# A mixture-of-experts layer: the rows of the expert slots turned by transposing DMAs instead of TensorE

## The chip, the cores and the metric

The kernel runs on one core of one Trainium2 chip. The metric is the device time of one execution in microseconds (us). The times are medians of several runs.

## The reference, cut to what matters

4096 tokens of 128 channels go through an attention-like block and a mixture of experts, each followed by a layer norm. What the change touches is the second half:

```python
x = _layernorm(x + attention(x))                      # called x1 below, [4096, 128]
logits = x @ gate_w                                   # 8 experts, 2 chosen for each token
top_v, top_i = top_k(logits, 2); top_p = softmax(top_v)
g = einsum('th,ehi->tei', x, Wg); u = einsum('th,ehi->tei', x, Wu)      # 352 inner columns
d = einsum('tei,eih->teh', silu(g) * u, Wd)
expert_out = einsum('te,teh->th', combine, d)         # combine holds top_p
shared = silu(x @ Sg) * (x @ Su) @ Sd                 # 176 inner columns
x = _layernorm(x + expert_out + shared)
```

Only the two chosen experts of a token are computed.

## The kernel before, in words

The work goes in four stages, and every engine has its own hand-written list of instructions with semaphores between them.

**Token loop.** 32 tiles of 128 tokens, in 38 steps (`for s in range(LAST_STEP + 1)` on each engine). The steps are software-pipelined: in step s VectorE masks tile s-1, adds x to tile s-2, TensorE transposes x1 of tile s-4 and forms the router's logits of tile s-5. x1 of a tile is written by ScalarE's `normalise` (L796) as fp32, twice, into `x1_rows[:, t, 0]` and `x1_rows[:, t, 1]`, one row of 132 words for each of the two chosen experts: 128 channels, the destination of the result (word 128) and the weight (word 129). TensorE transposes the first of them (`bank_p`, L580), ScalarE takes its high half in fp16 (`x1T_hi`, L778) and VectorE the remainder (`x1T_lo`, L1000); a value is then a sum of two fp16 numbers. VectorE's last work in a step is `rope_cos` (L920), its first in the next are the masks (L938). Every four tiles are a quad; VectorE chooses the experts of a quad and finds each row's place in DRAM, and GpSimd writes the rows there with indirect DMAs (`scatter`, L1288), one tile and one choice at a time, beginning eight steps after the quad's last tile entered. SyncE loads xT of tile t once tile t-4 is turned (L416).

**Shared expert and table.** In the last steps and behind them TensorE computes the shared expert (`shared_up`, `shared_down`), VectorE adds it to x1 into `x_sb` (`shared_add`, L1058), and makes the table of slot tiles (`table`). SyncE writes padding rows behind each expert's region.

**Expert loop.** The 8192 rows, sorted by expert in the DRAM tensor `rows`, are worked through in 39 slot tiles of 256 slots; the last few can be dummies. The instructions of four tiles form one round: ScalarE, VectorE, SyncE and GpSimd run the rounds in a hardware loop (the first two rounds are written out on the first three), TensorE's are all written out. For tile t:
- SyncE: `load` (L442) brings 256 rows of 528 bytes into `slot_rows[:, t % 4]`, once the buffer's previous tile has been turned and its meta copied.
- TensorE: `slot_turn` (L654) transposes the two blocks of 128 rows, fp32, into PSUM; ScalarE casts them to the high half (`slots_hi`, L861), VectorE subtracts for the low half (`evac`, L1174) and copies destination and weight to `slot_meta` (L1178). `slots_T` has two buffers.
- TensorE: `up` (L669 to L671), 18 matmuls of 256 columns in fp16, three for each of six blocks (high by high, low by high, high by low), once `slots_copied` says that the low half is there.
- ScalarE: `silu` three times (L869); VectorE: `hidden` three times (L1186).
- TensorE: `down` (L685), six fp32 matmuls in two passes each, once `hidden_done` says so and the one PSUM area `y_ps` has been read. ScalarE: `scale` (L880), two activations with the weight. GpSimd: `scatter_results` (L1321), two indirect DMAs to `ydram`.

The orders in the loop, which decide what stands behind what: TensorE does up(t), slot_turn(t+1), down(t-1). ScalarE does the three silus of t, slots_hi(t+1), scale(t-1). VectorE does the three hidden of t, evac(t+1).

**Final stage.** When the scatters of the real tiles have landed, SyncE loads the results of both choices (L452), they are added to `x_sb` on VectorE (L1217, L1219) or TensorE (L716 to L720), normalised and stored.

## Time and profile before

| | us |
|---|---|
| median of 3 runs | 424.5 (423.6 to 426.48) |
| the profiled execution | 426.87 |
| its span, first to last instruction | 425.0 |
| mean granted TensorE clock in it | 0.959 |

The times of instructions below come from the profiled execution and count from the start of its span. The granted clock is a share of the full 2.4 GHz. A matmul is pipelined, so the durations of neighbours overlap, and what one costs is the distance between starts.

### The profile page before, as it was taken

Reading aid. Unit: us, or ns where it says so; the run is one execution under the profiler, and the core shown is the slowest. Engines: PE = TensorE matmul, PEld = TensorE weight load, DVE = VectorE, ACT = ScalarE, POOL = GpSimd, SP = SyncE. Lnnn points to the kernel's source line nnn. Section 1 sums busy time; section 2 is a strip of 40 time slices with the busy share of each in tenths; the row PEclk is TensorE's granted clock in tenths of the full one; section 3 lists DMA queues with packets and bytes.
Section 4 is the critical chain, followed back from the end, with each engine's and each line's share of the span. In section 5 each row is a group of like instructions: output and inputs, shape, how many; then the busy total and the mean of one; then the engine's idle time right before and its main releaser. Section 6 shows DMA issues by size and latency. Waiting matters only on the chain.

```text
span 425.0 us, 12763 instructions
## 1 busy us (share of the span) xinstructions
PE 347.0 (82%) x4172; PEld 271.8 (64%) x4172; DVE 257.6 (61%) x826; ACT 235.0 (55%) x861; POOL 233.5 (55%) x302
## 2 busy tenths in 40 slices
PE   3798888787978887886489898897977979889980
PEld 2476656565756655645347797877977878779730
DVE  1469998978797879787555443333443433434682
ACT  3587779687877868523112354444454444445354
POOL 3377636768585868777640044534444345344682
PEclk9999999999899989999969999989999899899986
DMA  8956000101011110101232022212212222121784
GB/s 222 331 165 152 16 22 20 47 29 45 28 47 34 41 41 21 35 25 49 64 107 66 27 65 68 73 50 64 77 57 59 63 61 74 52 71 38 219 294 131
DMA packets 32280, 33.47 MB, mean 79 GB/s; under 512 B 4784, under 2 KB 27632, under 8 KB 32080
## 3 DMA queue, kind: packets, MB, share of 16 engines
q1 hardware_dynamic: 27360, 23.19, 18.9%
q0 software_dynamic: 4544, 9.45, 6.8%
q8 instruction: 36, 0.59, 0.6%
q14 instruction: 20, 0.16, 0.1%
q10 hardware_dynamic: 320, 0.08, 0.1%
HBM read 21.16 MB, written 13.56 MB: 82 GB/s over the span
## 4 chain that ended last, share of the span: by engine, by line
PE 51%; DVE 15%; issue 11%; ACT 10%; another core or an unknown queue 3%; POOL 3%; DMA 2%; SPq 2%; DVEq 1%; ACTq 0%; POOLq 0%
PE b_p L685 9%; PE b_es L671 6%; PE b_es L669 5%; PE b_es L670 4%; DVE masked_energies L938 4%; PE b_in L477 3%; PE b_es L502 3%; ACT turns L763 2%; PE b_es L514 2%; ACT ffn_staged L869 2%; PE b_o L534 2%; DMA x_rows<-ydram 2%; PE b_in L654 1%; PE b_o L528 1%
## 5 line engine op out<-in xcount | busy, mean ns | idle before, releaser
L1321 POOL DMA_INDIRECT ydram<-ffn_staged,slot_meta x78 | 74.9, 960 | 111.6 <-ACT ffn_staged L880 92.1
L1186 DVE TENSOR_TENSOR ffn_staged<-ffn_staged,b_es 128x256 f32<-128x256 f32 x79 | 31.8, 420 | 78.3 <-ACT ffn_staged L869 57.6
L1288 POOL DMA_INDIRECT rows<-x_rows,place x64 | 65.4, 1023 | 16.0 <-issue 13.6
L669 PE MATMUL b_es<-slots_T,w_hi 128*128 128x256 f16 x158 | 45.4, 287 | 19.2 <-DVE slots_T L1174 18.3
L685 PE MATMUL b_p<-w_down,ffn_staged 128*128 (+1 forms) x468 | 58.7, 275 | 1.0 <-issue 1.0
L685 PEld LDWEIGHTS b_p<-w_down,ffn_staged 128*128 128x128 f32 (+1 forms) x468 | 55.3, 191 | 1.2 <-issue 1.1
L869 ACT ACTIVATE ffn_staged<-b_es 128x256 f32<-128x256 f32 x79 | 29.2, 385 | 33.9 <-PE b_es L671 28.3
L763 ACT ACTIVATE turns<-b_turn,const_sb 128x128 f32<-128x128 f32 x128 | 36.5, 368 | 16.6 <-PE b_turn L488 15.9
L671 PE MATMUL b_es<-slots_T,w_lo 128*128 128x256 f16 x158 | 45.4, 287 | 0.0
L670 PE MATMUL b_es<-slots_T,w_hi 128*128 128x256 f16 x158 | 45.3, 287 | 0.0
L880 ACT ACTIVATE ffn_staged<-b_p,slot_meta 128x128 f32<-128x128 f32 x78 | 24.4, 366 | 35.9 <-PE b_p L685 34.1
L938 DVE TENSOR_TENSOR masked_energies<-b_es,const_sb 128x512 f32<-128x512 f32 x64 | 41.0, 680 | 1.8 <-PE b_es L502 1.4
L477 PE MATMUL b_in<-w_raw,xT_ring 128*128 128x384 f32 x64 | 30.6, 564 | 9.2 <-DMA ln_w_b<-in_ln 6.7
L796 ACT ACTIVATE x_rows<-x_plus,x_shift,rstd 128x256 f32<-128x256 f32 x32 | 19.2, 600 | 27.4 <-DVE x_shift L978 27.0
L1253 POOL TENSOR_TENSOR turned_qk<-qk,const_sb 128x256 f32<-128x256 f32 x32 | 26.2, 820 | 13.5 <-ACT qk L738 13.4
L669 PEld LDWEIGHTS b_es<-slots_T,w_hi 128*128 x158 | 16.0, 101 | 23.9 <-issue 21.3
L752 ACT ACTIVATE v_spread<-b_in 64x64 f32<-64x64 f32 x128 | 28.3, 221 | 1.1
L528 PEld LDWEIGHTS b_o<-turns,states 128*128 128x128 f32 x56 | 8.9, 196 | 30.9 <-DVE products L948 25.4
L1280 POOL TENSOR_TENSOR var_eps<-stat,const_sb 128x2 f32<-128x2 f32 x33 | 7.2, 219 | 36.4 <-ACT squares_out L788 36.1
L502 PE MATMUL b_es<-turns 32*64 32x128 f32 x1024 | 25.5, 286 | 1.7 <-issue 1.0
L920 DVE TENSOR_TENSOR roped<-qk,const_sb 128x256 f32<-128x256 f32 x32 | 23.0, 720 | 6.0 <-ACT qk L738 5.9
L528 PE MATMUL b_o<-turns,states 128*128 128x128 f32 x56 | 13.8, 330 | 15.2 <-DVE products L948 12.4
(213 smaller groups left out, 914.6 us busy)
## 6 DMA issues: line engine op xcount, KB each, us to landing
ffn_staged<-rows SPq DMA_DIRECT2D x39, 132.0 KB, 2.1
x_rows<-ydram SPq DMA_DIRECT2D x16, 256.0 KB, 6.8
xT_ring<-in_xT SPq DMA_DIRECT2D x32, 64.0 KB, 1.8
x_sb<-in_x SPq DMA_DIRECT2D x4, 512.0 KB, 6.1
out<-x_sb SPq DMA_DIRECT2D x8, 256.0 KB, 2.3
ffn_staged<-in_Wg SPq DMA_DIRECT2D x1, 1408.0 KB, 7.5
ffn_staged<-in_Wu SPq DMA_DIRECT2D x1, 1408.0 KB, 6.7
ydram<-ffn_staged,slot_meta POOLq DMA_INDIRECT x78
```

The lines of the kernel that those rows point to most:

```text
L477: nc.tensor.matmul(b_in[:, 0:3 * P], x_t, w_raw[:, :], start=True, stop=True).then_inc(projected, 1)
L502: mm = nc.tensor.matmul(b_es[H * h:H * h + H, g, P * c:P * c + P], keys[g], queries[g][:, 2 * h:2 * h + 2, H * c:H * c + H], start=True, s ...
L669: nc.tensor.matmul(o, w, slots_T[:, j % 2, 0, :], start=True, stop=False)
L670: nc.tensor.matmul(o, w, slots_T[:, j % 2, 1, :], start=False, stop=False)
L671: mm = nc.tensor.matmul(o, wlo, slots_T[:, j % 2, 0, :], start=False, stop=True)
L685: mm = nc.tensor.matmul(y_ps[:, b * P:(b + 1) * P], hidden_T[0:n, k % 2, c, b * P:(b + 1) * P], w_down_flat[0:n, bass.ds(e * (IC * P) + c ...
L763: nc.scalar.activation(turns[:, t % TR, j * P:(j + 1) * P], b_turn[:, P:2 * P], ACT.Copy, scale=C("spread")[:, j:j + 1])
L869: nc.scalar.activation(silu_gate[:, j % 2, c, :], up_banks[j % 2][c][:, 0:SLOTS], ACT.Silu).then_inc(expert_silu_done[c], 1)
L938: nc.vector.tensor_tensor(masked_energies[:, t % 2, 2 * r:2 * r + 2, :].rearrange("p c (b n) -> p c b n", n=H), b_es[:, 2 * r:2 * r + 2, 0 ...
L1186: ins = nc.vector.tensor_tensor(hidden_T[:, j % 2, c, :], silu_gate[:, j % 2, c, :], up_banks[j % 2][c][:, SLOTS:], ALU.mult)
L1288: nc.gpsimd.indirect_dma_start(out=rows, out_offset=bass.IndirectOffsetOnAxis(ap=place[:, t // R, c, t % R:t % R + 1], axis=0), in_=x1_row ...
L1321: nc.gpsimd.indirect_dma_start(out=ydram, out_offset=bass.IndirectOffsetOnAxis(ap=slot_meta[:, j, b, 0:1].bitcast(u32), axis=0), in_=scale ...
```

## The change

The rows in DRAM keep their 528 bytes, but the first 512 now hold a token's 128 high halves and 128 low halves in fp16 instead of 128 fp32 values. They are made in the token loop: ScalarE's `normalise` writes x1 in fp32 into `x_sb` and its fp16 cast into the row of the first choice, VectorE's new `rows_lo` writes the difference, and SyncE copies four tiles' rows at a time to the rows of the second choice. GpSimd's scatters wait for `rows_lo` and, for the second choice, for that copy. TensorE transposes x1 for the router and the shared expert from `x_sb`.

In the expert loop `slot_turn`, `slots_hi` and `evac` go. SyncE issues a transposing DMA straight into `slots_T`, which now has four buffers, and a second small DMA for `slot_meta`. `y_ps` gets a second area. The waits are redrawn: up(t) waits for the DMA and for hidden(t-2).

```diff
@@ SyncE, token loop @@
+            def turn_x1(t):
+                if not tile(t):
+                    return
+                sp.wait_ge(x1_lo_done, t + 1)
+                if t % R == R - 1:
+                    quad = x1_halves[:, t + 1 - R:t + 1, :, 0:2 * P]
+                    sp.dma_start(quad[:, :, 1, :], quad[:, :, 0, :]).then_inc(rows_doubled[t // R % 2], 16)
             for t in range(XR, TILES):
                 sp.wait_ge(turned, t - XR + 1)
                 sp.dma_start(xT_ring[:, t % XR, :], xT[:, t * P:(t + 1) * P]).then_inc(xT_loaded[t % XR], 16)
                 if t % 2 == 0:
                     load_ffn(t // 2 - XR // 2)
+                turn_x1(t - 7)
+            for t in range(TILES - 7, TILES):
+                turn_x1(t)
@@ SyncE, expert loop @@
                 if exists(t - U):
-                    sp.wait_ge(slots_turned, t - U + 1)
-                    sp.wait_ge(meta_copied, t - U + 1)
+                    sp.wait_ge(expert_up_done[IC - 1], t - U + 1)
                     sp.wait_ge(table_loaded, 16)
-                sp.dma_start(slot_rows[:, j, :, :], rows[bass.ds(at, SLOTS), :].rearrange("(p b) w -> p b w", p=P)).then_inc(slots_loaded[j], 16)
+                sp.dma_start_transpose(slots_T[:, j, :, :], row_halves[bass.ds(at, SLOTS), 0:2 * P]).then_inc(slots_loaded[j], 16)
+                if exists(t - U):
+                    sp.wait_ge(y_scattered[j], 32 * i)
+                    sp.wait_ge(table_loaded, 16)
+                sp.dma_start(slot_meta[:, j, :, :], rows[bass.ds(at, SLOTS), DEST:DEST + 2].rearrange("(b p) w -> p b w", p=P)).then_inc(meta_loaded[j], 16)
@@ TensorE @@
-                    last = nc.tensor.transpose(x1T_ps, x1_rows[:, s - 4, 0, 0:P], C("identity"))
+                    last = nc.tensor.transpose(x1T_ps, x_sb[:, s - 4, :], C("identity"))
...
-            def slot_turn(i, j, lag):
...
-                pe.wait_ge(slots_copied, t + 1)
+                pe.wait_ge(slots_loaded[j], 16 * (i + 1))
+                if exists(t - 2):
+                    pe.wait_ge(hidden_done, t - 1)
...
                 pe.wait_ge(hidden_done, t + 1)
-                if exists(t - 1):
-                    pe.wait_ge(yscaled[(j + lag - 1) % U], i + (j + lag - 1) // U + 1)
+                if exists(t - 2):
+                    pe.wait_ge(yscaled[(j + lag - 2) % U], i + (j + lag - 2) // U + 1)
...
-                slot_turn(i, j, 1)
                 down(i, j, -1, last_owner)
@@ ScalarE @@
-                both = x_plus[:, t % 2, :].unsqueeze(1).broadcast_to([P, TOP, P])
-                nc.scalar.activation(x1_rows[:, t, :, 0:P], both, ACT.Identity, scale=rstd[:, 1 - t % 2, 1:2], bias=x1_shift[:, t % 2:t % 2 + 1]).then_inc(x1_done, 1)
+                for to in (x_sb[:, t, :], x1_halves[:, t, 0, 0:P]):
+                    ins = nc.scalar.activation(to, x_plus[:, t % 2, :], ACT.Identity, scale=rstd[:, 1 - t % 2, 1:2], bias=x1_shift[:, t % 2:t % 2 + 1])
+                ins.then_inc(x1_done, 1)
...
-                slots_hi(i, j, 1)
                 scale(i, j, -1)
@@ VectorE @@
+            def rows_lo(t):
+                if not tile(t):
+                    return
+                dve.wait_ge(x1_done, t + 1)
+                nc.vector.tensor_tensor(x1_halves[:, t, 0, P:2 * P], x_sb[:, t, :], x1_halves[:, t, 0, 0:P], ALU.subtract).then_inc(x1_lo_done, 1)
...
                 rope_cos(s + 3)
+                rows_lo(s - 3)
...
-            def evac(i, j, lag):
...
@@ GpSimd @@
+                if t % R == 0 and c == 1:
+                    pool.wait_ge(rows_doubled[t // R % 2], 16 * (t // R // 2 + 1))
                 if t % R == 0 and c == 0:
                     pool.wait_ge(placed, t // R + 1); pool.wait_ge(weighed, t // R + 1); pool.wait_ge(destinations_set, 1)
+                    pool.wait_ge(x1_lo_done, t + R)
```

## Rows read from the trace of the kernel before

**Rows 1.** The page, part 1: busy time, share, instructions of TensorE.
```profile
PE 347.0 (82%) x4172; PEld 271.8 (64%) x4172; DVE 257.6 (61%) x826; ACT 235.0 (55%) x861; POOL 233.5 (55%) x302
```

**Rows 2.** Windows: us, busy us of each engine, granted clock, DMA share, GB/s.
```profile
60.00:100.00 40.00, 33.91 (x642) 25.03 (x632) 34.48 (x115) 31.75 (x136) 27.32 (x40) 1.00 0.11 33
...
270.00:290.00 20.00, 17.82 (x147) 15.97 (x147) 7.68 (x25) 8.77 (x28) 9.21 (x10) 0.91 0.20 58
290.00:310.00 20.00, 17.41 (x156) 16.02 (x154) 7.00 (x21) 8.60 (x28) 9.89 (x11) 1.00 0.24 67
```

**Rows 3.** Timeline of TensorE, 300 to 313 us: start, duration, what, idle before.
```profile
302.65 0.27 PE L669 MATMUL b_es<-slots_T,w_hi 128*128 128x256 f16 x1
...
304.61 0.38 PE L654 MATMUL b_in<-const_sb,ffn_staged 128*128 128x128 f32 x2
...
304.83 1.50 PE L685 MATMUL b_p<-w_down,ffn_staged 128*128 x12
...
306.17 0.27 PE L669 MATMUL b_es<-slots_T,w_hi 128*128 128x256 f16 x1
```

**Rows 4.** Timeline of VectorE, line L1174: tile 1, two in the middle, tile 34.
```profile
240.21 0.42 DVE L1174 TENSOR_TENSOR slots_T<-b_in,slots_T 128x256 f16<-128x256 f32 x1
...
305.57 0.42 DVE L1174 TENSOR_TENSOR slots_T<-b_in,slots_T 128x256 f16<-128x256 f32 x1
...
311.46 0.42 DVE L1174 TENSOR_TENSOR slots_T<-b_in,slots_T 128x256 f16<-128x256 f32 x1
...
380.07 0.42 DVE L1174 TENSOR_TENSOR slots_T<-b_in,slots_T 128x256 f16<-128x256 f32 x1 [0.32 <-ACT slots_T L861]
```

**Rows 5.** One gap in the timeline, and TensorE's waits, 236 to 402 us.
```profile
308.53 0.38 ACT L869 ACTIVATE ffn_staged<-b_es 128x256 f32<-128x256 f32 x1 [1.45 <-PE b_es L671]
...
309.94 0.38 ACT L869 ACTIVATE ffn_staged<-b_turn 128x256 f32<-128x256 f32 x1 [1.02 <-remote]
...
310.70 0.38 ACT L869 ACTIVATE ffn_staged<-b_o 128x256 f32<-128x256 f32 x1 [0.38 <-remote]
...
312.02 0.28 PE L669 MATMUL b_es<-slots_T,w_hi 128*128 128x256 f16 x1 [2.16 <-DVE slots_T L1174]
...
PE b_es L669 <- DVE slots_T L1174: 18.3, 9, 2.5
```

**Rows 6.** Timeline after a gap; DMA issues (KB, us to landing); scatters and a waiter.
```profile
277.93 0.42 PE L671 MATMUL b_es<-slots_T,w_lo 128*128 128x256 f16 x1
...
ffn_staged<-rows SPq DMA_DIRECT2D x39, 132.0 KB, 2.1
x_rows<-ydram SPq DMA_DIRECT2D x16, 256.0 KB, 6.8
...
L442 SPq DMA_DIRECT2D ffn_staged<-rows x39: 337/338/362, 226.3 to 380.8; - x39
...
309.10 0.96 POOL L1321 DMA_INDIRECT ydram<-ffn_staged,slot_meta  x1 [0.30 <-issue]
...
391.20 0.95 POOL L1321 DMA_INDIRECT ydram<-ffn_staged,slot_meta  x1 [0.30 <-issue]
...
394.97 0.22 DVE L1178 COPY slot_meta<-ffn_staged 128x4 int32<-128x4 int32 x1 [0.19 <-DMA ydram<-ffn_staged,slot_meta]
```

**Rows 7.** Groups (count, busy us, mean ns, idle before), VectorE's wait, timeline: token loop.
```profile
L1000 DVE TENSOR_TENSOR x1T<-b_p,x1T 128x128 f16<-128x128 f32 x32 | 9.1, 285 | 11.4 <-ACT x1T L778 10.5 <-ACT squares_out L788 0.5
...
DVE x1T L1000 <- ACT x1T L778: 10.5, 14, 1.4
...
L796 ACT ACTIVATE x_rows<-x_plus,x_shift,rstd 128x256 f32<-128x256 f32 x32 | 19.2, 600 | 27.4 <-DVE x_shift L978 27.0
...
L880 ACT ACTIVATE ffn_staged<-b_p,slot_meta 128x128 f32<-128x128 f32 x78 | 24.4, 366 | 35.9 <-PE b_p L685 34.1
...
116.45 0.60 ACT L796 ACTIVATE x_rows<-x_plus,x_shift,rstd 128x256 f32<-128x256 f32 x1
116.55 1.03 DVE L920 TENSOR_TENSOR roped<-qk,const_sb 128x256 f32<-128x256 f32 x1
```

More of the change, by code:

```diff
@@ L274, in build @@
         x1_done = sem("x1_done")
+        x1_lo_done = sem("x1_lo_done")
         x1T_hi_done = sem("x1T_hi_done")
         x1T_lo_done = sem("x1T_lo_done")
+        rows_doubled = [sem(f"rows_doubled{k}") for k in range(2)]
         logits_read = sem("logits_read")
@@ L326, in build @@
         slots_loaded = [sem(f"slots_loaded{k}") for k in range(U)]
+        meta_loaded = [sem(f"meta_loaded{k}") for k in range(U)]
         rows_scattered = [sem(f"rows_scattered{k}") for k in range(R)]
@@ L643, in _ @@
                     shared_up(q + 2)
-            def slot_turn(i, j, lag):
-                ok, t, k, r = stage(i, j, lag)
-                if not ok:
-                    return
-                pe.wait_ge(slots_loaded[k], 16 * (r + 1))
-                if exists(t - 1):
-                    pe.wait_ge(slots_copied, t)
-                for b in range(2):
-                    mm = nc.tensor.transpose(slots_T_ps[:, b * P:(b + 1) * P], slot_rows[:, k, b, 0:P], C("identity"))
-                mm.then_inc(slots_turned, 1)
             def expert_of(t):
@@ L853, in _ @@
                 shared(q)
-            def slots_hi(i, j, lag):
-                ok, t, k, r = stage(i, j, lag)
-                if not ok:
-                    return
-                act.wait_ge(slots_turned, t + 1)
-                nc.scalar.activation(slots_T[:, k % 2, 0, :], slots_T_ps, ACT.Copy).then_inc(slots_hi_done, 1)
             def silu(i, j, c):
@@ L879, in scale @@
                 for b in range(2):
[L880 removed]
+                    ins = nc.scalar.activation(scaled_y[:, k, b, :], y_ps[k % 2][:, b * P:(b + 1) * P], ACT.Copy, scale=slot_meta[:, k, b, 1:2])
                 ins.then_inc(yscaled[k], 1)
[L883 removed]
             def experts(i, j):
```

44 lines of the change are left out of this document (13 added, 31 removed).

## The prediction

> **What bounds the kernel now.** I read the page first. Over the whole span TensorE is the busiest engine, 82% [rows 1], but that is an average over two stages, so next come the windows. In the token loop (about 20 to 208 us) VectorE is busy 34.5 us of 40 and TensorE 33.9: both are near a bound. In the expert loop (about 237 to 401 us) VectorE, ScalarE and GpSimd are under half busy, TensorE at about 87% [rows 2]. So in the expert loop what counts is TensorE's own work and its idle gaps.
>
> The timeline of TensorE shows one slot tile: first up matmul at 302.65, the two turns of the next tile's rows at 304.61, the twelve passes of down at 304.83, the next tile at 306.17 [rows 3]. A tile takes 3.52 us with no gap: up 1.96, turns 0.22, down 1.34. But L1174, which runs once per tile, starts at 240.21 for tile 1 and at 380.07 for tile 34: 33 tiles in 139.86 us [rows 4]. At 3.52 each they would take 116.2, so 23.7 us are something else. The starts 305.57 and 311.46 show where: most tiles come at 3.5, but every fourth one at about 5.9; there are 8 such gaps. In this one ScalarE does silu at 308.53, 309.94 and 310.70, after idle times of 1.45, 1.02 and 0.38 us though its matmuls were done before 308.3: 2.85 us of stall, called "remote" in part [rows 5]. I read it as ScalarE waiting for its own instructions once per round of four tiles; that is an inference from the period. The cast of the next tile's rows (L861) stands behind these silus in ScalarE's order, L1174 behind it, the next up behind that, and TensorE idles 2.16 us at 312.02. The waits sum it: 18.3 us in 9 waits for L1174 [rows 5]. After some of these gaps the granted clock falls to the lower level (1.2 GHz) for one up: a matmul of it takes 0.42 us where the same one takes 0.27, and the window reads 0.91 [rows 2, 3, 6]. Three gaps of about 5.1 us are such ones; they follow the idling and belong to the 23.7.
>
> **Part 1, the turn leaves TensorE, ScalarE and VectorE.** Per tile two transposes of together 0.22 us go, so TensorE's own period becomes 3.30. The last real tile is tile 34 (the loads of the results at L452 start once its scatter has landed), so 34 periods count: 34 x 0.22 = 7.5 us. The casts L861 and L1174 and the copy L1178 also go; they were beside other work, and count only through the stalls.
>
> **Part 2, the stalls lose their path to TensorE.** Afterwards up of tile t+1 waits for its transposed slots and for hidden of tile t-1, no longer for anything ScalarE does behind silu of tile t. Down of tile t waits for hidden of tile t, but it stands behind up of t+1: it is due one whole period, 3.30 us, after the last matmul of its own up has been issued. In the stalled tile up ended at 308.13 (306.17 and 1.96) and hidden can end near 311.5, a multiplication behind the silu of 310.70, that is 3.4 us: 0.1 late instead of 2.2. So almost the whole of the stalls is hidden, and with the idling goes the lower clock: up to 23.7 us. What is late next is scale (L880) of the previous tile, by about 1.5 us, with it the scatter, and with it the next transposing DMA (part 3). I give back 0.5 us per stall, 8 x 0.5 = 4 us. Part 2: -19.7 us.
>
> **Part 3, the transposing DMA and SyncE's queue.** SyncE now issues two DMAs per tile in one order: the transpose of tile t (waits for up of t-4), then the slot_meta load, which waits until the scatter of t-4 has landed. Behind that wait stands the transpose of t+1. Count from the end of up of tile t-4, with period T. Down of t-4 follows up of t-3, at +T. From there to the start of its second scatter were 4.49 us (304.61 to 309.10), 4.27 without the turns [rows 3, 6]. Its landing: no row gives it cleanly; the load of the same rows lands 2.1 us after issue, and the scatter issued at 391.20 released its waiter at 394.97, 3.8 us [rows 6]. I take 3.0. With 0.4 for the meta load's issue (a load of rows holds the queue 0.34 [rows 6]) the transpose of t+1 is issued at T + 7.6. Up of t+1 wants it at 4T + 1.34. It may thus take D = 3 x 3.30 + 1.34 - 7.6 = 3.6 us from issue to landing. If it takes longer, the ring of five tiles sets the period: T = (9.56 + D) / 4.
>
> D is the unknown; no row of before has a transposing DMA. Below: the plain load of as many rows, 2.1 us. Above: the loads of results, 256 KB, 6.8 us [rows 6], which have twice the bytes and fifteen others beside them. I take 3.0, nearer to the plain load, because the destination is of the same size and DMA engines are busy only about a fifth of this stage. That is under 3.6, so it costs nothing but the 4 us above. The meta load itself (256 pieces of 8 bytes) is due at scale, some 5 us later than it lands. The first four transposes are issued without such waits around 226 us and are due from 237 us.
>
> The page "VectorE: DVE Perf Modes" of the Trainium skill, section "The three transpose paths", speaks against this: it gives a 128x128 transpose through the DMA crossbar as 1309 ns. A tile here is four such blocks; as an estimate from that page, one behind the other, 5.2 us, which by the formula is a period of 3.69. The skill's page "DMA: Bandwidth & Descriptors", section "Latency and other measured facts", gives 261 GB/s for transposing DMAs, by which the 128 KB would add 0.5 us, and D would stay near the plain load. No trace here decides between them.
>
> **Part 4, the token loop pays.** VectorE gets rows_lo, 32 times: its twin L1000, the same subtraction from PSUM, takes 0.29 us [rows 7]. It stands last in the step, behind rope_cos. Its new wait, for ScalarE's normalise of the same step, is met in the timeline: normalise runs 116.45 to 117.05, rope_cos until 117.58 [rows 7]. Behind it stand the masks, for which TensorE's attend waits. VectorE also waits itself, 10.5 us in this loop for L778 [rows 7] and less elsewhere, so part of the 32 x 0.29 = 9.3 us is swallowed; it is busy 86%, and I take 60%: 5.5 us. ScalarE's normalise, 0.60 for 256 columns [rows 7], becomes two of 128. A 128-column activation from PSUM is 0.37 (L880) [rows 7], so two take 0.74 or less: 0.1 more each time, 3 to 4 us of ScalarE in all, of which TensorE's transpose of x1 (L580), which waits for normalise, feels a part: 1 us. TensorE's transpose of x1 reads other rows of the same shape: nothing. The doubling copy, 8 times on SyncE's queue, is issued about four steps (20 us) before its scatter is due, and the xT load behind it is due a step later than it comes: nothing. If that cover failed it would be about 2 us for each, 16 us. Bounds of part 4: 0 (all swallowed) to 32 x (0.29 + 0.15) = 14 us. Together +6.5.
>
> **Sum.** For the profiled execution, 426.9 us with a span of 425.0: -7.5 - 19.7 + 6.5 = -20.7, giving 406.2. It stands 2.4 above the median of 424.5, so the median becomes 403.8; I say 404.
>
> **Rivals.**
> A, the transposing DMA is slow (other side). Mechanism: D above 3.6 makes the ring through SyncE the bound. With D = 6.8, T = 4.09: 34 x (4.09 - 3.52) = +19.4; of the stalls, which now delay the scatter within the ring, I let half go, -11.9; the token loop +6.5; sum +14, 438.5 us. Slower begins where 34 x (T - 3.52) exceeds 5.4, at T = 3.68, D = 5.2. For it: the ring is tight, 1.5 us above a plain load; TensorE's idling would bring the lower clock on top. Against: DMA engines have room. 18%.
> B, the ring binds mildly, D between 3.6 and 5.2: T of 3.29 to 3.69, 406 to 424, with D = 4.4 giving T = 3.49: -1.0 - 11.9 + 6.5, 418 us. 15%.
> C, the stalls are not absorbed: they also hit GpSimd's or SyncE's loop, or hold TensorE through hidden. Then -7.5 + 6.5, 423.5 us. For it: they recur in every round, and all these loops wrap at the same tiles. Against: the slack of 3.3 us is counted above. 7%.
> D, the token loop takes the full 14 us: 411.5. For it: VectorE's 86%. 5%.
> That the edit does not do what it says, I give no weight: the turns are gone from the code.
>
> **How the numbers follow.** The forecast holds 55%. A change of under 1% (4.2 us) can't be told from none here. Faster by over 1%: 55 + 5 + most of B (13) = 73%. Within 1%: C's 7, 2 of B, and 1 of A: 10%. Slower: 17%. The range: at the low end part 4 costs nothing and the stalls go wholly, 424.5 - 7.5 - 23.7 = 393.3, so 393. Above it must take in B, C and the milder half of A: 430.
>
> **What would show it.** Right: in the expert loop the first up matmuls (L669) of neighbouring tiles stand 3.30 us apart, also across ScalarE's "remote" idle times; TensorE's waits on L669 sum to under 5 us; granted clock near 1.00; landing of the transposing DMA under 3.6 us; in the token loop a VectorE group of 32 with about 0.29 us and a loop longer by 6 us. Wrong: L669 waiting for slots_T from a DMA, landing times above 5 us; TensorE waiting for hidden (L1186) at each fourth tile; or a token loop longer by 14 us.

## The result, and the profile after

The changed kernel takes 427.58 us in the median (422.96 to 432.19, 20 runs), the kernel before, on the same chip, 424.5 (420.17 to 433.64, 20 runs). The ratio is 1.0087, with a 95% interval of 1.0059 to 1.0116: a loss of 0.9%, where a gain of 5% was forecast. Some executions of a kernel are slow, a per cent or two longer at a lower granted clock; ratios and their intervals, here and below, are of the fast ones alone, medians of all. The profiled execution of the changed kernel was a long one (432.19 us, span 430.4); its second profile, of a0_again below, has a span of 429.5.

The page, part 1, of the changed kernel, then windows over the stretches of [rows 2] (us, busy us of each engine with instructions, granted clock, DMA share, GB/s):

```profile
PE 347.3 (81%) x4094; PEld 266.2 (62%) x4094; DVE 250.7 (58%) x780; ACT 228.8 (53%) x854; POOL 233.9 (54%) x302
```

```profile
60.00:100.00 40.00, 31.98 (x585) 23.08 (x585) 35.42 (x111) 32.51 (x139) 25.07 (x39) 1.00 0.15 43
270.00:290.00 20.00, 17.74 (x154) 15.69 (x153) 6.53 (x17) 8.90 (x29) 9.11 (x10) 1.00 0.34 68
290.00:310.00 20.00, 18.10 (x162) 16.35 (x160) 5.21 (x13) 7.12 (x22) 10.08 (x11) 1.00 0.31 70
```

TensorE has 78 instructions fewer, two turns for each of 39 tiles. In the token loop VectorE is busier than in [rows 2] (35.42 against 34.48 of 40 us) while TensorE does less in the same 40 us (31.98 against 33.91): the loop is slower. In the expert loop TensorE is as busy as before, although its tile is shorter.

The token loop. First its groups in the changed kernel (count, busy us, mean ns, idle before), then the last masked product of the loop in its timeline and in that of the kernel before:

```profile
L799 ACT ACTIVATE x_sb<-x_plus,x_shift,rstd 128x128 f32<-128x128 f32 x30 | 14.8, 493 | 28.4 <-DVE x_shift L971 26.8 <-issue 1.2
L799 ACT ACTIVATE x_rows<-x_plus,x_shift,rstd 128x128 f16<-128x128 f32 x30 | 14.3, 478 | 0.0
L542 PE MATMUL b_o<-turns,states 128*128 128x128 f32 x56 | 14.2, 338 | 17.4 <-DVE products L941 17.4
...
L1000 DVE TENSOR_TENSOR x_rows<-x_sb,x_rows 128x128 f16<-128x128 f32 x30 | 11.3, 378 | 1.0 <-ACT x_rows L799 1.0
```

```profile
194.65 0.41 DVE L941 TENSOR_TENSOR products<-b_es,const_sb 128x256 f32<-128x256 f32 x1
```

```profile
182.57 0.41 DVE L948 TENSOR_TENSOR products<-b_es,const_sb 128x256 f32<-128x256 f32 x1
```

The loop ends 12.1 us later. TensorE's attend (L542) waits 17.4 us for VectorE's products, where it waited 12.4 before. rows_lo (L1000) has a mean of 0.378 us, not the 0.29 of its twin in [rows 7], but that mean mixes two durations. In a0_again 26 of the 32 take 0.26 to 0.29 us, one takes 0.43, and five take 0.81; these five, four tiles apart, are those that run beside GpSimd's L1240, which then takes 0.93 us instead of 0.73. From VectorE's and GpSimd's timelines of a0_again:

```profile
68.23 0.29 DVE L1000 TENSOR_TENSOR x_rows<-x_sb,x_rows 128x128 f16<-128x128 f32 x1 [0.30 <-ACT x_rows L799]
73.38 0.81 DVE L1000 TENSOR_TENSOR x_rows<-x_sb,x_rows 128x128 f16<-128x128 f32 x1
...
66.90 0.72 POOL L1240 TENSOR_TENSOR turned_qk<-qk,const_sb 128x256 f32<-128x256 f32 x1
73.11 0.93 POOL L1240 TENSOR_TENSOR turned_qk<-qk,const_sb 128x256 f32<-128x256 f32 x1
```

The expert loop. TensorE's timeline at the first up of four neighbouring tiles, then the waits of 240 to 370 us (us in total, times, longest) and SyncE's timeline:

```profile
282.37 0.28 PE L673 MATMUL b_es<-slots_T,w_hi 128*128 128x256 f16 x1 [0.64 <-DMA slots_T<-rows]
...
285.68 0.27 PE L673 MATMUL b_es<-slots_T,w_hi 128*128 128x256 f16 x1
...
289.56 0.28 PE L673 MATMUL b_es<-slots_T,w_hi 128*128 128x256 f16 x1 [0.41 <-DMA slots_T<-rows]
...
293.57 0.28 PE L673 MATMUL b_es<-slots_T,w_hi 128*128 128x256 f16 x1 [0.53 <-DMA slots_T<-rows]
```

```profile
ACT ffn_staged L865 <- remote: 25.9, 12, 3.4
...
PE b_es L673 <- DMA slots_T<-rows: 8.3, 12, 2.2
```

```profile
278.12 0.40 SPq L456 DMA_DIRECT2D slot_meta<-rows  x1
279.48 1.22 SPq L452 DMA_TRANSPOSE slots_T<-rows  x1
280.95 0.38 SPq L456 DMA_DIRECT2D slot_meta<-rows  x1
```

The first distance is 3.31 us, as forecast for a tile without turns; the next are 3.88 and 4.01. ScalarE's waits that the profile calls remote, which the prediction expected to lose their effect, are longer than before (in the same window 13.1 us in 13 waits there, the longest 1.8). So here is the balance, by the first up matmul of tiles 0, 1 and 34 in a0_again (251.13, 253.38, 379.56; span 429.5) and in the kernel before (237.29, 240.77, 380.64; span 425.0). The expert loop starts 13.8 us later; tiles 0 to 1 give back 1.2, tiles 1 to 34 another 13.7 (33 times 3.824 us against 4.238); and behind tile 34 another 5.6 us go. Together +4.5. The loop was to give back 27 us and gave 15.

Part of the 15 is the clock. These are the windows of 240 to 370 us, of the kernel before and of a0_again:

```profile
240.00:370.00 130.00, 113.86 (x978) 103.77 (x979) 50.29 (x155) 60.05 (x183) 55.88 (x59) 0.96 0.22 63
240.00:370.00 130.00, 118.59 (x1003) 102.88 (x1002) 41.85 (x102) 51.33 (x158) 55.84 (x59) 1.00 0.31 63
```

The kernel before has three ups at the lower level (distances of 5.20, 5.20 and 5.07 us), which cost it 4.9 us against 3.53; a0_again has none. Without them, what its tiles 1 to 34 take beyond the stall-free periods measured below (3.526 and 3.307 us) is 18.6 us before and 17.1 us in a0_again: the stalls themselves hardly shrank.

### The profile page after: what moved, and what is told of

It is laid out like the page before. It is cut to its first block, busy times and chain, and to the rows that moved or that the text cites. A ratio compares the mean times of both kernels' runs of the same rounds, so it can differ in the third digit from the quotient of the medians.

```text
span 430.4 us, 12627 instructions
## 1 busy us (share of the span) xinstructions
PE 347.3 (81%) x4094; PEld 266.2 (62%) x4094; DVE 250.7 (58%) x780; ACT 228.8 (53%) x854; POOL 233.9 (54%) x302
## 4 chain that ended last, share of the span: by engine, by line
PE 28%; DVE 18%; issue 18%; SPq 14%; ACT 8%; DMA 7%; POOL 4%; another core or an unknown queue 1%; DVEq 1%; ACTq 0%; POOLq 0%
SPq L452 5%; DVE masked_energies L931 3%; SPq L447 3%; DMA ydram<-ffn_staged,slot_meta 3%; SPq L456 3%; PE b_es L516 3%; ACT turns L766 2%; PE b_in L491 2%; DMA slots_T<-rows 2%; PE b_o L548 2%; PE b_es L528 2%; POOL ydram L1311 2%; DVE roped L913 2%; PE b_o L542 2%; PE b_p L689 1%
## 5 line engine op out<-in xcount | busy, mean ns | idle before, releaser
L673 PE MATMUL b_es<-slots_T,w_hi 128*128 128x256 f16 x158 | 43.5, 276 | 11.5 <-DMA slots_T<-rows 9.1
L766 ACT ACTIVATE turns<-b_turn,const_sb 128x128 f32<-128x128 f32 x128 | 36.6, 369 | 13.4 <-PE b_turn L502 11.8
L675 PE MATMUL b_es<-slots_T,w_lo 128*128 128x256 f16 x158 | 43.3, 274 | 0.0
L674 PE MATMUL b_es<-slots_T,w_hi 128*128 128x256 f16 x158 | 43.3, 274 | 0.0
L865 ACT ACTIVATE ffn_staged<-b_es 128x256 f32<-128x256 f32 x79 | 27.4, 395 | 21.1 <-PE b_es L675 16.4
L799 ACT ACTIVATE x_sb<-x_plus,x_shift,rstd 128x128 f32<-128x128 f32 x32 | 15.8, 493 | 33.9 <-DVE x_shift L971 32.3
L1240 POOL TENSOR_TENSOR turned_qk<-qk,const_sb 128x256 f32<-128x256 f32 x32 | 25.8, 806 | 13.4 <-ACT qk L741 13.3
L689 PE MATMUL b_in<-w_down,ffn_staged 128*128 (+1 forms) x228 | 29.4, 278 | 2.7 <-DVE ffn_staged L1175 2.7
L689 PE MATMUL b_p<-w_down,ffn_staged 128*128 (+1 forms) x240 | 31.1, 281 | 0.0
L516 PE MATMUL b_es<-turns 32*64 32x128 f32 x1024 | 28.5, 293 | 3.0 <-issue 2.5
L689 PEld LDWEIGHTS b_in<-w_down,ffn_staged 128*128 128x128 f32 (+1 forms) x228 | 27.0, 191 | 5.0 <-issue 4.8
L542 PEld LDWEIGHTS b_o<-turns,states 128*128 128x128 f32 x56 | 9.2, 201 | 33.5 <-DVE products L941 33.4
L689 PEld LDWEIGHTS b_p<-w_down,ffn_staged 128*128 128x128 f32 (+1 forms) x240 | 29.5, 197 | 0.3
L542 PE MATMUL b_o<-turns,states 128*128 128x128 f32 x56 | 14.2, 338 | 17.4 <-DVE products L941 17.4
L1175 DVE TENSOR_TENSOR ffn_staged<-ffn_staged,b_turn 128x256 f32<-128x256 f32 x19 | 8.0, 421 | 34.2 <-ACT ffn_staged L865 25.6
```

What stands on the lines that cost most here:

```text
L516: mm = nc.tensor.matmul(b_es[H * h:H * h + H, g, P * c:P * c + P], keys[g], queries[g][:, 2 * h:2 * h + 2, H * c:H * c + H], start=True, s ...
L542: nc.tensor.matmul(outT, states[:, t % SR, :], qT, start=True, stop=False, skip_group_check=True)
L673: nc.tensor.matmul(o, w, slots_T[:, j, 0, :], start=True, stop=False)
L674: nc.tensor.matmul(o, w, slots_T[:, j, 1, :], start=False, stop=False)
L675: mm = nc.tensor.matmul(o, wlo, slots_T[:, j, 0, :], start=False, stop=True)
L689: mm = nc.tensor.matmul(y_ps[k % 2][:, b * P:(b + 1) * P], hidden_T[0:n, k % 2, c, b * P:(b + 1) * P], w_down_flat[0:n, bass.ds(e * (IC * ...
```

## The experiments

Eighteen kernels ran, in five groups on four chips, each group beside the kernel before on the same chip. That had medians of 425.17 us (a0, a2, b1, b3), 428.55 (c), 430.76 (d), 432.21 (e, b2) and 425.92 (f), so times are compared inside a group, or by their ratio. Seven of them are probes and not kernels to use: those with plain stores (c1, c4, d3, d4, d5) or fixed target rows (e3) leave out that results go to their tokens' rows, and c3 leaves out that each tile has its own expert.

### Is it the ring through SyncE?

**a0_again**, the changed kernel once more, for an ordinary execution.

> The changed kernel itself, for a second trace. Both theories of its time expect the same here: 1.01 of the kernel before (about 427 us), token loop 12 us longer than before, slot tiles 3.8 to 3.9 us apart on average. If the distance of 6.3 us between tiles 16 to 18 of the first trace is part of the kernel, it is there again; if it was an accident of that execution, the average falls to about 3.75.

Measured: 427.65 us, ratio 1.0109 (1.0063 to 1.0155). The two distances of 6.31 and 6.17 us that the first profile had behind tiles 16 and 17, with a granted clock of 0.83 in the window of 310 to 330 us, are not there, and the average is 3.824 instead of 3.885: chance, and no cause of the loss.

**a2_lag** takes the small load out of the next transpose's way:

```
                 sp.dma_start_transpose(slots_T[:, j, :, :], ...)      # tile t
-                sp.wait_ge(y_scattered[j], 32 * i)
-                sp.dma_start(slot_meta[:, j, :, :], ...)              # tile t
+                sp.wait_ge(y_scattered[k], 32 * r)
+                sp.dma_start(slot_meta[:, k, :, :], ...)              # tile t - 1
```

(Cut: the arguments, and the conditions for the first and last tiles.)

> Changed kernel, with the slot_meta load of a tile issued one tile later on SyncE's queue, behind the transpose of the next tile, so that no transpose stands behind the newest wait for a scatter. Theory 1 (the ring through SyncE's order sets the period: scatter landed, slot_meta, next transpose): the period falls from 3.88 to about 3.4, 34 tiles x 0.45 = 15 us faster than the changed kernel, about 412 us, 0.97 of before. Theory 2 (the transposing DMA is itself too slow or the DMA engines too full): nothing changes, 427 us. Theory 3 (ScalarE's stalls reach TensorE through hidden): nothing or a few us, 424 to 427.

Measured: 427.64 us, ratio 1.0087 (1.0044 to 1.013). The transposes now land 2 to 4 us ahead of their use in most tiles, and TensorE waits for one once, for 1.1 us; yet the ups are 3.77 us apart, and TensorE's down waits 5.9 us in 12 waits for hidden. The ring does not set the period. My first theory of the miss fell with this run.

### Is it the order of the engines, or the token part?

**b1_reorder** is the kernel before (no transposing DMA) with the next tile's turn ahead of up on TensorE, its cast ahead of the silus on ScalarE and its subtraction ahead of the hidden products on VectorE (the small copy to slot_meta stays behind them). TensorE's part:

```
+                slot_turn(i, j, 1)
                 if exists(t):
                     ...
                     up(i, j, owner[j])
-                slot_turn(i, j, 1)
                 down(i, j, -1, last_owner)
```

> Kernel before, with the turn of the next tile's rows put ahead of up on TensorE, and its cast ahead of the silus on ScalarE and its subtraction ahead of hidden on VectorE; no transposing DMA, nothing new in the token loop. If the 23.7 us of gaps are ScalarE's stalls, reaching TensorE only because the cast stands behind the stalled silus (as the prediction had it): the gaps close, period 3.52 to 3.6, 18 to 22 us faster, about 404 us, 0.955 of before. If the stalls reach TensorE also through hidden or y_ps: less than half of it, 415 us or more. If the stall sits wherever the loop wraps and now hits the cast itself: no gain, 424 us.

Measured: 410.85 us, ratio 0.9636 (0.9548 to 0.9725). It beats both kernels, but not by what a stall-free loop would: distances now alternate between 3.53 and 3.8 to 4.4, 3.80 on average. The stall of every fourth tile has become one of every second.

**b3_token** is the kernel before with the token part of the change alone (two normalisations, rows_lo, the doubling copies, with a spare tile for the low halves).

> Kernel before with the token part of the change alone: normalise as two activations (fp32 row, fp16 spare), the subtraction on VectorE into a spare tile, the doubling copies on SyncE and the scatters' waits; the expert loop as before. Theory 1 (the token loop costs 12 us and the expert loop gives 10 back): 436 us, 1.028 of before. If the token loop's 12 us in the changed kernel come from elsewhere (its first trace being a long execution): 430 us or less, and the expert loop then gives little back.

Measured: 434.84 us, ratio 1.0135 (1.0025 to 1.0245); its last product stands at 194.32, 11.8 us later than before.

**b2_dve** keeps of that only the one VectorE operation, from an input that is there anyway:

```
+                nc.vector.tensor_tensor(x1_spare[:, t % 4, 1, :], x1_rows[:, t, 0, 0:P], half[:, 0:P], ALU.subtract).then_inc(x1_lo_done, 1)
```

> The kernel before with one more VectorE operation for each token tile: the 128 x 128 subtraction of the changed kernel's low halves, from the same input, into a spare tile, and nothing else of the token part. b3_token (all of the token part) took 5.7 us more than the kernel before by the ratio. If VectorE's time sets the token loop: most of that here, +4 to +6 us. If the second normalisation on ScalarE and the waits for it do: +0 to +2 us.

Measured: 439.49 us, ratio 1.0267 (1.0138 to 1.0396). That is more than either theory gave, and more than b3_token's 1.0135, which contains this operation; the two intervals overlap, so the ratios do not split the token part. The last product stands at 193.08, 10.5 us later than before. One profile's token loop is good to about 3 us only: it ends between 179.6 and 185.5 in the twelve profiles that leave it as it was (182.57 is the kernel before), and between 194.2 and 197.0 in the seven with the whole token part. The 32 new operations take 11.7 us together (mean 0.366, again five of 0.81 beside the same instruction of GpSimd). So most of the token part's 12.1 us is this one instruction, and most of its time goes onto the loop.

### What stalls the expert loop

The trace also keeps the times of semaphore updates. TensorE's increments tell ScalarE that a block of up is done; I matched the three of each up with the modelled end of the matmul that carries each. Where nothing is held up they agree to 0.01 us, so that lateness can be read directly. In the kernels with a stall the matmuls are started on time, and their increments come late. (Traces of kernels with scatters lack some updates, and a missing one looks like a late one. b1_reorder has all updates of these three semaphores, and ScalarE's waits end with them.)

Three kernels, all on top of b1_reorder, took one suspect each. **c2_unroll** writes out the loops of ScalarE and VectorE.

> b1_reorder with ScalarE's and VectorE's expert loops written out for all 35 tiles instead of a hardware loop of four tiles a pass; the work is the same. In b1_reorder the ups are 3.80 us apart on average where two ups without a stall are 3.53 apart, so 34 x 0.27 = 9 us are in the stalls that come with every second tile. Theory L (the stall is code that ScalarE or VectorE fetches in its loop): no stalls, 402 us, the waits of ScalarE called remote gone. Theory S (TensorE's semaphore increments are delivered late while GpSimd writes the descriptors of the scatters or while these move data) and theory V (TensorE's own register loads hold its increments back): 411 us, the waits as in b1_reorder.

**c3_noload** fixes the expert, so that TensorE loads no registers.

> b1_reorder with the expert of every tile taken as 0 on TensorE, so that no register is loaded from SBUF there and the weights stand at fixed places (the outputs of the experts are left wrong by that; the number of matmuls is the same). Theory V (the register loads of TensorE hold back its increments and its issue): no stalls, ups 3.3 to 3.5 us apart, 398 to 402 us. Theories S and L: 411 us, increments still up to 3 us late every second tile.

**c1_plainstore** and **c4_poolstore** replace the indirect scatters by plain stores to fixed rows, c1 on SyncE's queue, c4 on GpSimd with its loop written out. c4's edit:

```
-                    nc.gpsimd.indirect_dma_start(out=ydram, out_offset=bass.IndirectOffsetOnAxis(ap=slot_meta[:, j, b, 0:1].bitcast(u32), axis=0),
-                                                 in_=scaled_y[:, j, b, :], in_offset=None).then_inc(y_scattered[j], 16)
+                    nc.gpsimd.dma_start(ydram[SLOTS * t + b * P:SLOTS * t + b * P + P, :], scaled_y[:, j, b, :]).then_inc(y_scattered[j], 16)
```

> b1_reorder with the two scatters of a tile, which GpSimd issues, replaced by two plain stores of the same bytes to fixed rows, which SyncE issues behind its loads (the results of the experts are not put to their tokens' rows). Theory S in either form (GpSimd's descriptor writing, or its 8 KB of small writes, delays TensorE's increments): no stalls, 402 us. If what delays is the DMA traffic into DRAM itself, the stalls stay: 411 us. Theories L and V: 411 us.

> b1_reorder with the two scatters of a tile replaced by two plain stores of the same bytes to fixed rows, issued by GpSimd in the same places of its program (the results are not put to their tokens' rows). Theory S, form 1 (what delays TensorE's increments is GpSimd as the issuer): the stalls stay, 411 us, while c1_plainstore has none. Theory S, form 2 (the reading of the scatter's indices, one descriptor for each row): no stalls here either, 402 us. Theories L and V: 411 us.

Measured: c2_unroll 413.88, 414.41, 422.23 and 653.53 us, the last without an explanation, against 428.55 (no interval), 49.5 us of remote waits, the stalls as in b1_reorder. c3_noload 408.63 us, ratio 0.9538 (0.9468 to 0.9609): the stalls begin at tile 10 instead of 5 and then come every second tile all the same, 3.71 us on average; register loads have a small part at most. c4_poolstore 402.66 us, ratio 0.9348 (0.9229 to 0.9466), and c1_plainstore 410.99, ratio 0.9603 (0.953 to 0.9675): in both no wait between 240 and 370 us is called remote any more and **every distance from tile 1 to tile 34 is 3.52 or 3.53 us**. (What c1_plainstore then loses against c4_poolstore is behind the loop, where VectorE waits 10.9 us for a load of the results that stands behind SyncE's stores.) The DMA packets of c4_poolstore and b1_reorder are the same in number and bytes, so it is not the amount of traffic.

In the timeline of b1_reorder GpSimd issues four scatters in a row and ScalarE waits for increments of matmuls long issued; in that of c4_poolstore the same silus follow at 0.66 us:

```profile
255.34 0.96 POOL L1328 DMA_INDIRECT ydram<-ffn_staged,slot_meta  x1 [0.30 <-issue]
256.60 0.96 POOL L1328 DMA_INDIRECT ydram<-ffn_staged,slot_meta  x1 [0.30 <-issue]
```

```profile
257.10 0.38 ACT L869 ACTIVATE ffn_staged<-b_es 128x256 f32<-128x256 f32 x1 [2.27 <-remote]
258.53 0.66 ACT L869 ACTIVATE ffn_staged<-b_es 128x256 f32<-128x256 f32 x2 [1.05 <-remote]
```

```profile
265.03 0.39 ACT L869 ACTIVATE ffn_staged<-b_es 128x256 f32<-128x256 f32 x1
265.69 0.38 ACT L869 ACTIVATE ffn_staged<-b_es 128x256 f32<-128x256 f32 x1 [0.27 <-PE b_es L671]
266.34 0.38 ACT L869 ACTIVATE ffn_staged<-b_es 128x256 f32<-128x256 f32 x1 [0.27 <-PE b_es L671]
```

Worked out from the update times (us; due is the modelled end of the matmul, late what the increment comes after it):

```
               three increments due      late               scatters issued from this up to the next
before
tile 16   303.47 304.12 304.78    0.07 0.01 0.01     304.87, 306.13
tile 17   306.99 307.64 308.30    1.46 2.27 2.38     307.83, 309.10
b1_reorder
tile 5    250.95 251.60 252.26    0.22 0.01 0.01     252.81
tile 6    254.77 255.42 256.08    2.25 3.08 2.51     254.07, 255.34, 256.60
tile 7    258.29 259.16 259.82    0.54 0.01 0.01     260.46, 261.71
tile 8    262.60 263.26 263.91    2.09 2.93 2.36     262.98, 264.24
c4_poolstore
tile 6    257.94 258.60 259.25    0.01 0.01 0.01     (plain) 258.26, 258.79
tile 7    261.47 262.12 262.78    0.01 0.01 0.01     (plain) 261.79, 262.32
```

Tile 17 of the kernel before is the stall of [rows 5]: its increments come at 308.45, 309.91 and 310.68, and the three silus start at 308.53, 309.94 and 310.70. There two pairs of scatters stand 0.75 us apart. In tile 6 of b1_reorder four stand 0.30 apart; the first increment comes at 257.01 and the second at 258.50, 1.7 and 1.9 us after the issue of the third and the fourth. The late increments make ScalarE late, its results come together, GpSimd gets two pairs at once, and these four scatters hold the next increments: so, as I read the timelines, the stall feeds itself, every second tile. Which increment is held, and for how long, I can't give as a rule: in e1_gate below one due 0.82 us after the first scatter of a pair came on time (281.86), and one due 0.22 us after the second came 1.35 us late.

c4_poolstore changed two things, the kind of DMA and GpSimd's loop. **d1_poolflat** writes out the loop and keeps the scatters.

> b1_reorder with GpSimd's loop over the expert tiles written out, its 78 scatters kept as they are. c4_poolstore changed two things at once: the scatters became plain stores, and GpSimd's loop of four tiles a pass was written out; its ups then stood 3.53 us apart without a stall. If the hardware loop of GpSimd is what holds TensorE's increments back: no stalls here, ups 3.53 apart, 402 us. If it is the indirect DMA: stalls every second tile as in b1_reorder, 411 us.

Measured: 418.5 us (414.16 to 422.21) against 430.76 of the kernel before (four runs, with no interval), 50.0 us of remote waits, 3.87 us on average. GpSimd's loop is not the cause.

**e3_fixed** keeps the indirect form but names 128 consecutive rows by a table made once.

> d1_poolflat with the scatters' indices taken from a table made once, which name 128 consecutive rows, so that the indirect DMAs write what c4_poolstore's plain stores write (the results are not put to their tokens' rows; the last 14 stores, of tiles 32 to 38, are plain). If the indirect form itself holds back TensorE's increments: stalls every second tile up to tile 31, ups 3.8 us apart, 415 us. If the scattered target rows do it: ups 3.53 apart, 403 us.

Measured: 410.25 us, ratio 0.9573 (0.9443 to 0.9702), distances of 3.53 and 4.0 to 4.3 in turn from tile 6 to tile 34, and of 3.53 again at tiles 35 and 36, behind the first plain stores. This is its wait, to be held against none in c4_poolstore:

```profile
ACT ffn_staged L871 <- remote: 45.0, 27, 2.4
```

So the indirect form of the instruction does it, not the scattered rows. An indirect DMA also keeps GpSimd busy for 0.96 us where the plain one takes 0.54; no run separates the form from that time.

### The two kernels of the case without that stall

**d4_before_plain**, **d3_after_plain** and **d5_lag_plain** are the kernel before, the changed kernel and a2_lag with the same plain stores.

> The kernel before with the same plain stores. If the scatters make its stall of every fourth tile: ups 3.53 us apart against 4.24, 34 x 0.71 = 24 us, so about 401 us, ScalarE's waits called remote gone. If ScalarE's order makes the stall, as the prediction said: 425 us.

> The changed kernel with GpSimd's scatters of the experts' results replaced by plain stores of the same bytes to fixed rows (the results are not put to their tokens' rows), GpSimd's loop written out. If the scatters are all that stalls the changed kernel: ups 3.31 us apart against 3.85, 34 x 0.54 = 18 us, so 409 us. If the ring through SyncE still sets a part: ups 3.5 to 3.75 apart, 415 to 424 us, TensorE waiting for slots_T.

> a2_lag (the changed kernel, the load of slot_meta issued one tile later) with the same plain stores. Without the scatters' stalls and with the transposes early: ups 3.31 us apart against 3.77, 34 x 0.46 = 16 us, so 411 us, no wait of TensorE for slots_T. That the stalls stay (427 us) would mean that the transposing DMAs or the small loads cause them too.

Measured side by side, three runs each: 407.58 us (before, 400.47 to 407.8, no interval), 415.28 (changed, 410.05 to 417.02, ratio 0.9614, 0.9477 to 0.975) and 412.63 (changed, with the lag, 407.92 to 414.18, ratio 0.9558, 0.943 to 0.9687), the kernel before itself 430.76. Average distances: 3.526, 3.348 and 3.307 us. TensorE's timeline of the first ups of three tiles, of d4_before_plain and of d5_lag_plain, and the landing of d3_after_plain's DMAs (KB each, median us from issue to landing):

```profile
273.21 0.27 PE L669 MATMUL b_es<-slots_T,w_hi 128*128 128x256 f16 x1
...
276.74 0.27 PE L669 MATMUL b_es<-slots_T,w_hi 128*128 128x256 f16 x1
...
280.26 0.27 PE L669 MATMUL b_es<-slots_T,w_hi 128*128 128x256 f16 x1
```

```profile
274.67 0.27 PE L682 MATMUL b_es<-slots_T,w_hi 128*128 128x256 f16 x1
...
277.98 0.27 PE L682 MATMUL b_es<-slots_T,w_hi 128*128 128x256 f16 x1
...
281.28 0.27 PE L682 MATMUL b_es<-slots_T,w_hi 128*128 128x256 f16 x1
```

```profile
slots_T<-rows SPq DMA_TRANSPOSE x39, 2.7
slot_meta<-rows SPq DMA_DIRECT2D x39, 2.0 KB, 1.9
```

The kernel before has no stall left either: its stall of every fourth tile was the scatters' too. And the changed kernel, freed of the stall, is still 5 to 8 us slower in the median than the kernel before so freed, and 7 to 10 us by the fastest run of each. By the profiles (spans 405.7, 415.2 and 410.8) its expert loop starts 11.6 us later, 10.9 with the lag; tiles 0 to 34 give back 7.1 and 8.5; and behind tile 34 it takes 5.0 and 2.7 us more. The transposing DMA does save its 0.2 us a tile; the token loop and the end cost more.

### Placing the scatters

**e1_gate** and **e2_spread** keep real scatters on b1_reorder's order and only choose when they are issued; GpSimd's loop is written out in these and in f1 and f2, as in d1_poolflat. e2_spread:

```
             pool.wait_ge(table_made, 1); pool.wait_ge(yscaled[j], n)
             for b in range(2):
+                if b == 1:
+                    pool.wait_ge(hidden_done, min(t + 3, SLOT_TILES))
```

> d1_poolflat with the pair of scatters of tile t also waiting for TensorE's second increment of up of tile t + 2, so that a pair starts 1.3 us after an up starts and the pairs stand 3.53 us apart, each 2.2 us long. If only four scatters in a row hold the increments back: no stalls, 402 to 405 us. If a pair by itself does too, where an increment falls into its end: stalls of every or every second tile, 411 us or more.

> d1_poolflat with the second scatter of tile t also waiting for VectorE's last hidden product of tile t + 2 (2.8 us after the up starts), so that no two scatters stand back to back: 1 us of scatter and 0.8 us of pause in turn. If back-to-back scatters are needed for the hold: no stalls, 402 us. If each scatter holds increments for a while: stalls of under 0.5 us in many tiles, 408 us or more.

Measured: e1_gate 410.14 us (405.97 to 414.11) against 432.21 (four runs, with no interval), distances of 3.53 with four of 4.5 to 5.1 among them, 3.65 on average; increments up to 1.35 us late in most tiles, which ScalarE's slack takes up. e2_spread 409.31 us, ratio 0.9567 (0.9438 to 0.9697), 3.53 without a break up to tile 30 and 3.59 on average. A pair alone holds increments back as well, but shortly; single scatters with a pause between them (0.66 us and more in f1_before_spread below, up to tile 26) do not visibly: there the ups stand 3.53 us apart, and of the 66 increments of tiles 5 to 26 49 are on time, while the other 17 are not in the trace.

**f1_before_spread** is the kernel before with that one wait, **f2_lag_spread** is a2_lag with it.

> The kernel before with GpSimd's expert loop written out and the second scatter of tile t waiting for VectorE's last hidden product of tile t + 2, as in e2_spread; nothing else. If back-to-back scatters are what stalls it: ups 3.53 to 3.65 us apart against 4.24, a ratio of 0.94 to 0.95, so 400 to 407 us by the chip. If the order of e2_spread's other engines is needed for it: above 0.96.

> a2_lag (the changed kernel, the load of slot_meta one tile later) with the same one wait. Its ups may stand 3.31 apart, which gains 34 x 0.22 = 7.5 us on f1_before_spread, and its token loop and start of the expert loop cost 11 to 13 us more: 4 to 6 us above f1_before_spread, a ratio to the kernel before of 0.955 to 0.965. If the stalls partly stay (the tile is shorter, so that scatters of 1 us and pauses fit less well): 0.97 or more.

Measured: f1_before_spread 405.37 us (404.18 to 409.27, six runs), ratio 0.9572 (0.9515 to 0.963). **One wait on GpSimd takes 4.3% off the kernel before**; it beats both kernels of the case, and reordering adds nothing to it that could be measured. (The loop written out, which comes with the wait, gained nothing in d1_poolflat.) GpSimd's timeline in it, with the pauses between the scatters:

```profile
262.69 0.96 POOL L1323 DMA_INDIRECT ydram<-ffn_staged,slot_meta  x1 [0.74 <-DVE ffn_staged L1186]
264.52 0.96 POOL L1323 DMA_INDIRECT ydram<-ffn_staged,slot_meta  x1 [0.87 <-ACT ffn_staged L880]
266.22 0.96 POOL L1323 DMA_INDIRECT ydram<-ffn_staged,slot_meta  x1 [0.74 <-DVE ffn_staged L1186]
268.12 0.96 POOL L1323 DMA_INDIRECT ydram<-ffn_staged,slot_meta  x1 [0.95 <-ACT ffn_staged L880]
```

Its distances are 3.53 up to tile 27 and then up to 4.8. From 330.60 us on its scatters stand 0.3 to 0.5 us apart in twos and threes again, and in tile 30 an increment comes 1.7 us late; what brings them together was not tried. f2_lag_spread took 422.02 us (twelve runs), ratio 0.9996 (0.9953 to 1.0039), a miss: its ups stand 3.31 apart for the first eight tiles and 3.70 on average. In a tile of 3.31 us the same waits leave shorter pauses, scatters stand 0.30 us apart again from tile 7 on, and the stall is back:

```profile
ACT ffn_staged L874 <- remote: 22.8, 11, 3.8
ACT ffn_staged L885 <- remote: 13.5, 4, 3.6
```

## Why the prediction was wrong

**Part 1, the turns leave TensorE: right.** Forecast 3.30 us instead of 3.52 a tile; measured 3.307 and 3.526 in d5_lag_plain and d4_before_plain, which over 33 distances is 7.2 us (forecast 7.5 over 34).

**Part 2, the stalls go: this is the step that failed.** It said that ScalarE waited for its own instructions, once in a round of four tiles, and that TensorE, no longer needing ScalarE's cast, would run on through it: -19.7 us. The remote waits in [rows 5] were waits for TensorE's increments, held back by indirect DMAs that came in two pairs close together; with plain stores in their place (d4_before_plain) the stalls are gone. The change left the scatters as they were, so the cause stayed. It was not absorbed either: with the shorter tile it came about every second tile in place of every fourth, in waits of up to 3.5 us in place of 1.8, and from there reached TensorE's down through hidden. The forecast's 27.2 us over 34 tiles meant an average of 3.44; it fell from 4.24 only to 3.82, and 33 x 0.38 = 12.5 us are the miss. In the terms of the sum: tiles 1 to 34 gave back 13.7 us, of which 7.2 are the turns of part 1 and 6.5 are what came of the 19.7. Of these 6.5 us 4.9 are the three ups at the lower clock, which a0_again does not have, and only 1.6 the stalls (18.6 to 17.1 us). That the clock would recover was forecast, but as a result of the idling going, and the idling stayed. The page had shown the pattern: [rows 6] has a scatter 0.30 us behind another at the gap of [rows 5], and I used it only to time the way from down to the scatter.

**Part 3, the ring through SyncE at no cost: right in its end, off in its terms.** The transposing DMA landed in 2.7 us (taken 3.0). But issuing it takes 1.22 us as a rule, and from the small load's issue to the next transpose's 1.2 to 2.5 us pass, apart from one wait at the start, where 0.4 was assumed. Without the stalls the ring costs 3.348 - 3.307 = 0.04 us a tile, 1.4 us in all; with them, TensorE waits 8.3 us for slots_T in the changed kernel, yet a2_lag without those waits is no faster. The Trainium skill's figure for transposing by DMA ("VectorE: DVE Perf Modes", "The three transpose paths"), from which the prediction had worked out 5.2 us for this size, would have made the ring bind; the traces have 2.7. That is near the plain load's 2.1 and the 0.5 us that would come to it, as an estimate, by the bandwidth of 261 GB/s in the Trainium skill's "DMA: Bandwidth & Descriptors", "Latency and other measured facts". One cost was missed: behind tile 34 the changed kernel takes 5.6 us more. SyncE issues its last small load at 395.41 in a0_again and the loads of the results from 398.27 on, which in the kernel before start at 395.09, since there nothing stands ahead of them that waits for a scatter to land. Without the scatters the two ends differ too: 5.0 us in d3_after_plain, 2.7 in d5_lag_plain. That this queue is the cause was read from the timelines and not tried by itself.

**Part 4, the token loop: right in direction, mis-sized.** Forecast +6.5 with 0 to 14 as bounds, measured +12.1, within about 3 us by the spread of the profiles. rows_lo was taken at 32 x 0.29 = 9.3 us with 60% of it on the path, 5.5; in a0_again it takes 11.9 us together, 2.6 of the difference in the five that ran beside GpSimd's L1240, and b2_dve alone lengthens the loop by 10.5. So the duration and the share on the path were both too small, about alike. VectorE's waits of [rows 7] did not swallow it: TensorE's attend waits 17.4 us for products L941 where it waited 12.4. Normalising took 0.88 us from its start to its end where 0.70 was forecast.

**The sum** with the measured terms, for a0_again against the profile before: +12.4 for the token loop (its last product stands at 194.96 there) and 1.5 more until the expert loop starts, -14.9 in it, +5.6 behind it: +4.6, where -20.7 had been forecast. Of the rivals, C (the stalls are not absorbed) came true in its mechanism and nearly in its size, and D (the token loop takes the full 14 us) nearly; I had given them 7% and 5% and had not added them together, which with D's 14 us would have made 424.5 - 7.5 + 14 = 431, and with the measured 12.1 us 429. Rivals A and B, on the transposing DMA, had 33% between them and were both wrong. That the range of 393 to 430 took in the result is no merit of the mechanism: its upper end of 430 was set for a slow transposing DMA.

## What to carry over

A wait that the profile calls remote is a wait whose releaser it did not find; look at what every other engine does in just those microseconds, GpSimd's DMAs too, before deciding that the waiting engine is its own cause. If increments of one engine come late while GpSimd issues indirect DMAs in a row, put a pause between these by waiting on something that ends in mid-tile: here that one wait was worth 18 us, two and a half times the 7 us of the turns on TensorE. It is tuned to a tile of 3.53 us and did not carry over to one of 3.31. An operation added at the end of a step of an engine that is 86% busy should be counted at its whole duration until shown otherwise. And a group's mean can hide two durations: look at single ones, and at what runs beside the long ones.

## What the runs showed of the hardware

- While GpSimd issues indirect DMAs close together (0.96 us each, 0.30 us between two, 0.30 to 0.75 between pairs), semaphore increments of TensorE are delivered up to 3.2 us late in b1_reorder, in a bunch, while the matmuls behind them go on being issued. Plain DMAs of the same bytes from the same engine (0.54 us each) delay them by 0.01 us at most. The indirect form does this with consecutive target rows too. Whether increments of other engines are delayed, and what the 64 scatters of the token loop cost, was not worked out. The Trainium skill tells ("DMA: Bandwidth & Descriptors", "SWDGE vs HWDGE vs iDMA") that GpSimd writes the descriptors of its DMAs into rings in SBUF. That these rings are the mechanism no run here shows. What holds the increments stays open.
- A transposing DMA of a 256 x 256 tile of 2-byte values occupies SyncE's queue for 1.22 us as a rule and lands 2.7 us after its issue, a plain load of 2 KB in 1.9 us (medians in d3_after_plain and d5_lag_plain).
- A 128 x 128 subtraction on VectorE with both inputs in SBUF took 0.26 to 0.29 us in 26 of 32 cases in a0_again, the same as with one input from PSUM (0.285, [rows 7]). It took 0.81 us in the five that ran beside GpSimd's operation of 128 x 256 (L1240), and that took 0.93 us instead of 0.73. b2_dve, b3_token and the first profile have the same five. Why these two hold each other up no run here separates.
